# Forming the fourth power table in the modulation's loop, and sending its first loads without TensorE's count

## The chip, the cores and the metric

The kernel runs on one core of one Trainium2 chip. The metric is the device time of one execution in microseconds; the number for a kernel is the median of its runs. The profile is one more execution, recorded by the hardware profiler.

## What is computed

One transformer block over 4096 rows of 512 channels with a context of 3202 rows of 384 channels, in float32, followed by a quantised feed-forward with a convolution. The part that matters here:

```python
# c_t: attention over the context, top 32 of each row, averaged over 4 heads
x = layernorm(x_text, g_norm_in, b_norm_in)
scale_in, shift_in = jnp.split(c_t @ W_film_in + b_film_in, 2, axis=-1)
x = x * (1.0 + mod_gate * scale_in) + mod_gate * shift_in      # the modulation
# s4d: y = causal convolution of x with K, per channel, plus x * D_skip
dt = jnp.exp(log_dt)
A = A_re + 1j * A_im
dtA = dt[:, None] * A
dC = C * (jnp.exp(dtA) - 1.0) / A
powers = jnp.exp(dtA[:, :, None] * jnp.arange(L))
K = 2.0 * jnp.einsum('dn,dnl->dl', dC, powers).real
```

The kernel never forms all powers: for a part of 32 channels (16 pairs of channels, 64 states, real and imaginary part) it keeps a "power table" of the powers 0 to 128, and carries states from chunk to chunk of 128 rows. There are 16 such parts.

## The kernel before

The program is a row of stages with a barrier of all engines between most of them: `prepare`, `attention` with `modulate` in the same block, `s4d`, `feed_forward`, `bit_feed_forward`. Each engine has its own instruction stream, written out in order; semaphores (`wait_ge`, `then_inc`) are all that orders them against each other. SP's stream issues most DMAs, and its waits hold back every DMA that stands behind them.

**attention** works on 32 tiles of 128 rows. Its last steps: VectorE adds the heads of the last tile (L932, then L936, which raises `last_summed`), GpSimd's adds of the heads are L808 to L819, TensorE transposes the sum (L1106, raising `turned`) and multiplies with the context (L1116), ScalarE copies the product into `u` (L998) and stores it to `scratch_u` (L1001, raising `u_stored`).

**modulate** works on the same 32 tiles, two buffers each for u and xt. For tile n:
- SP loads `u` (L1225) after TensorE's count `u_turned` and `xt` (L1227) after VectorE's count `x_read`. `u_turned` and `x_read` are raised by 2 at the start of TensorE's and VectorE's own streams of this stage.
- TensorE turns u (L1380). ScalarE makes the high half of u in float32r (L1361), VectorE the low half (`low_u`, L1308).
- TensorE multiplies three combinations of high and low halves with the film weights (L1393, 9 products for each of two halves) and adds `fb_parts` (L1396).
- VectorE takes the row statistics of xt (L1302, L1304), ScalarE the root (L1357), VectorE the reciprocal (L1313), then `film`: L1315 with the first half and L1318 with the second, which writes X by channel and raises `film_read`.

In VectorE's stream each round is `low_u` and `stats_of` of the next tile and then `film` of this one. Rounds stand in a loop of two tiles (`Fori`). Ahead of the loop VectorE makes `wf_parts` (L1324 to L1333) and `fb_parts` from GpSimd's `fbg` (L1337, L1339), and only then the first `low_u`. `fbg` is made by GpSimd (L1255 to L1258) from `fb`, which SP loads (L1234) behind the first four loads of u and xt. Then SP loads `W` and `root` (L1236, L1237).

Meanwhile GpSimd forms `powers` and the first three power tables (L1265 to L1288). One step of a table is two products with W (L1275), a drain, a difference and a sum (L1278, L1279), a drain. A table has 12 steps: one of width 1 for power 128, then widths 1, 2, 4 and 8, and seven steps of 16 columns (levels of 16, 32 and 64 columns go in pieces of 16).

**s4d** goes over 16 parts. TensorE: `gather(g)` (turns table g, sums the kernel, gathers the input of each chunk), `spread(g)` (output). The order is gather 0, gather 1, then gather g + 2 and spread g. VectorE: `table(3)` first, then `carry(0, 1)` and `carry(1, 1)`, then for each pair of parts a table, a carry (L1624 to L1656) over both, a table. There are four table buffers, so `table(g)` waits for the output of part g - 4. `carry` waits for ScalarE's copies of the gathered input (`U_copied`, L1699).

Of the kernel before, what the change touches and what calls it, by code (L numbers as in the profile page):

```python
# [8 lines left out]
F32 = mybir.dt.float32  # L9
BF16 = mybir.dt.bfloat16  # L10
F32R = mybir.dt.float32r
I32 = mybir.dt.int32
U8 = mybir.dt.uint8
ALU = mybir.AluOpType
# [3 lines left out]
P = 128  # L18
# [47 lines left out]
def after(m, b):  # L66

    return (m + 1, 0) if b else (m, 1)
# [1111 lines left out]
def modulate(nc, sem, block, attended, const, a, W, root_table, powers, first_tables, X, dram, wide, passed_on):  # L1180
# [5 lines left out]
    with scope:  # L1186
        u = sb("mod_u", [P, 2, DV])
        xt = sb("mod_xt", [P, 2, D])
        minus = sb("mod_minus", [P, P])
        minus_r = sb("mod_minus_r", [P, P], F32R)  # L1190
# [4 lines left out]
        rstd = sb("mod_rstd", [P, 2])  # L1195
        uT = sb("mod_uT", [P, 2, 2, VC, P], F32R)
        M = sb("mod_M", [P, 2, 2, GP, PIECE])
        sb("mod_gap", [P, 1088])
        wf_parts = sb("mod_wf_parts", [P, 2, VC, 2 * D], F32R)
        fb_high = sb("mod_fb_high", [2, 2 * D], F32R)  # L1200
        fb_parts = sb("mod_fb_parts", [P, 2 * D], F32R)
        part = sb("mod_part", [P, 2, D])
        fb = part.rearrange("p b d -> p (b d)")[0:2]
# [15 lines left out]
        def _(sp):  # L1219
            def load(m, b):  # L1220
                n = 2 * m + b
                sp.wait_ge(s["u_turned"], n + 1)
                if n >= TILES - 4:
                    sp.wait_ge(attended["u_stored"], 16 * (n + 2))
                sp.dma_start(u[:, b], dram["u"][n * P:(n + 1) * P, :]).then_inc(s[f"uin{b}"], 16)  # L1225
                sp.wait_ge(s["x_read"], n + 1)
                sp.dma_start(xt[:, b], a["x_turned"][n * P:(n + 1) * P, :]).then_inc(s[f"xin{b}"], 16)  # L1227

            sp.wait_ge(attended["summed"], SCORE_CHUNKS * (TILES - 1))
# [3 lines left out]
            sp.wait_ge(attended["last_summed"], SCORE_CHUNKS)  # L1233
            sp.dma_start(fb[:], dram["fb"][1, :].partition_broadcast(2)).then_inc(s["fb_in"], 16)  # L1234
            sp.wait_ge(attended["turned"], SCORE_CHUNKS * TILES)
# [6 lines left out]
        def _(pool):  # L1242
            nc.gpsimd.memset(eps2[:], EPS * EPS)
# [4 lines left out]
            pool.wait_ge(attended["last_summed"], SCORE_CHUNKS)  # L1248
# [9 lines left out]
            nc.gpsimd.tensor_tensor(fbg[0:2, D:2 * D], fbg[0:2, D:2 * D], fb[:, D:2 * D], ALU.add).then_inc(s["fb_scaled"], 1)  # L1258
            pool.wait_ge(attended["turned"], SCORE_CHUNKS * TILES)
# [23 lines left out]
            for t, Q in enumerate(first_tables):  # L1283
# [13 lines left out]
        def _(dve):  # L1297
# [8 lines left out]
            def low_u(m, b):  # L1306
                dve.wait_ge(s["uT_high"], 2 * m + b + 1)
                nc.vector.tensor_tensor(uT[:, b, 1], tp[b][:, :, ::-1], uT[:, b, 0].bitcast(F32), ALU.subtract).then_inc(s["uT_ready"], 1)  # L1308
# [28 lines left out]
            nc.vector.tensor_copy(fb_high[:], fbg[0:2])  # L1337
            dve.drain()
            nc.vector.scalar_tensor_tensor(fb_parts[0:2], fb_high[:].bitcast(F32), is_low[:, 0:1], fbg[0:2], ALU.mult, ALU.subtract).then_inc(s["fb_ready"], 1)  # L1339
            low_u(0, 0)  # L1340
            stats_of(0, 0)
            with dve.Fori(0, TILES // 2 - 1) as i:
                for b in range(2):
                    low_u(*after(i, b))
                    stats_of(*after(i, b))
                    film(i, b)
            low_u(TILES // 2 - 1, 1)
            stats_of(TILES // 2 - 1, 1)
            film(TILES // 2 - 1, 0)
# [85 lines left out]
def s4d(nc, sem, const, a, W, root, powers, first_tables, X, dram, wide, passed_on):  # L1435
# [15 lines left out]
    with scope:  # L1451
        Q = first_tables + [sb("s4_Q3", [P, 2, GP, P + 1])]
# [36 lines left out]
        with nc.Block() as block:  # L1489
# [84 lines left out]
            def _(dve):  # L1574
# [98 lines left out]
                dve.sem_inc(s["Q_ready"], 3)  # L1673
                table(3)
# [1608 lines left out]
def xattn_ffn(nc, a, out):  # L3283
    whole = ExitStack()
    with whole:
# [60 lines left out]
        with nc.Block() as block:  # L3346
# [9 lines left out]
            first_tables.append(third_table)  # L3356
            modulate(nc, sem, block, attended, const, a, W, root, powers, first_tables, X, dram, wide, passed_on)
# [58 lines left out]
```

## Time and profile before

| | us |
|---|---|
| median of 3 runs (3888.87 to 3891.64) | 3889.6 |
| the profiled execution | 3883.47 |
| its span, first to last instruction | 3881.7 |

In the profiled execution attention runs until about 1810 us, the modulation from about 1809 to 1978, and s4d from 1979 to about 2470. A row of the order of time gives the start and the length of an instruction, or of several alike in a row (x7), and in brackets how long its engine stood idle before, and what released it. Names ending in q (SPq, ACTq) are the engine's own queue issuing a DMA.

### The profile page before, as it was taken

The numbers are of one execution on the slowest core, as the hardware profiler recorded it, in microseconds if no ns is written. First come the engines' busy times: TensorE is split into PE (matmuls) and PEld (weight loads), VectorE is DVE, ScalarE is ACT, GpSimd is POOL, SyncE is SP. The second block draws the span as 40 slices with busy tenths as digits, with TensorE's granted clock in tenths as the row PEclk, the third lists the DMA queues.
The fourth block names the chain that finished last, engine by engine and source line by source line (L and its number), as shares of the span: only waits on it lengthen the run. The fifth ranks groups of instructions, "written<-read, shape, count | busy, mean of one in ns | idle before, by whom it ended". The sixth has DMA issues, their size and how long they took to land. (4 is left out here: it accounts for less than half of the span.)

```text
span 3881.7 us, 54514 instructions
## 1 busy us (share of the span) xinstructions
PE 3191.9 (82%) x17202; PEld 2127.3 (55%) x17202; DVE 2952.2 (76%) x7412; ACT 2275.6 (59%) x2934; POOL 1625.6 (42%) x1324
## 2 busy tenths in 40 slices
PE   7648758887878578887998777689999999978998
PEld 3224334444444244445865555467777777766776
DVE  7799999999999999996668998434444434468898
ACT  4578778898888698883133333133333223357876
POOL 0025546565555365665810000013332333317775
PEclk9758878788888787888999998899999999989999
DMA  9710000000000000002224333633444333430212
GB/s 321 259 47 11 10 8 10 10 10 10 12 10 10 5 13 10 10 5 83 94 58 98 82 92 82 195 121 126 133 133 133 128 103 117 143 97 15 67 50 70
DMA packets 262025, 290.53 MB, mean 75 GB/s; under 512 B 53264, under 2 KB 175782, under 8 KB 260588
## 3 DMA queue, kind: packets, MB, share of 16 engines
q1 hardware_dynamic: 245320, 262.39, 22.1%
q0 software_dynamic: 3040, 14.94, 1.0%
q10 hardware_dynamic: 13380, 10.00, 0.8%
q8 instruction: 106, 1.74, 0.2%
q14 instruction: 179, 1.47, 0.1%
HBM read 218.82 MB, written 68.45 MB: 74 GB/s over the span
## 5 line engine op out<-in xcount | busy, mean ns | idle before, releaser
L1116 PE MATMUL up<-ctx,attnT 128*128 128x384 f32 (+1 forms) x1664 | 718.8, 588 | 44.0 <-ACT attnT L988 43.9
L1086 PE MATMUL score<-KT,q 64*128 64x512 f32 (+1 forms) x1792 | 386.9, 527 | 330.1 <-ACT S L948 240.1
L849 DVE MAX8 both_wide<-S 128x8 f32<-128x146 f32 (+1 forms) x2816 | 601.2, 295 | 43.8 <-ACT S L948 25.0
L808 POOL TENSOR_TENSOR S<-S 128x512 f32<-128x512 f32 (+1 forms) x224 | 424.5, 1927 | 355.0 <-DVE S L854 355.0
L1116 PEld LDWEIGHTS up<-ctx,attnT 128*128 128x128 f32 (+1 forms) x1664 | 367.6, 231 | 319.6 <-issue 158.8
L854 DVE SCALAR_TENSOR_TENSOR S<-S,both_wide 128x3202 f32<-128x3202 f32 x128 | 472.8, 3756 | 14.6 <-ACT both_wide L979 14.6
L1086 PEld LDWEIGHTS score<-KT,q 64*128 64x128 f32 x1792 | 175.7, 239 | 531.9 <-ACT S L948 396.0
L948 ACT ACTIVATE S<-score 128x1024 f32<-128x1024 f32 (+1 forms) x448 | 403.1, 931 | 91.6 <-PE score L1086 91.1
L2301 DVE TENSOR_TENSOR ff_gelu<-ff_whole,ff_gelu 128x512 fp32r<-128x512 f32 x128 | 100.6, 786 | 417.3 <-ACT ff_gelu L2538 417.3
L957 ACT ACTIVATE both_wide<-S,below 128x3202 bf16<-128x3202 f32 x128 | 379.6, 2966 | 41.3 <-DVE below L889 20.4
L979 ACT ACTIVATE both_wide<-S,ebias 128x3202 f32<-128x3202 f32 x128 | 376.2, 2963 | 23.9 <-DVE S L854 13.5
L2705 PE MATMUL both_acc<-ff_W,ff_gelu 128*128 128x512 f32 x1000 | 336.7, 397 | 0.0
L2537 ACT ACTIVATE ff_whole<-both_hidden,ff_b 128x512 f32<-128x512 f32 x128 | 87.8, 686 | 389.5 <-PE both_hidden L2690 389.2
L2690 PE MATMUL both_hidden<-ff_hT,both_W 128*128 128x512 f32 x1024 | 264.7, 400 | 5.8 <-ACT ff_gelu L2538 4.3
L815 POOL TENSOR_TENSOR S<-S 128x512 f32<-128x512 f32 (+1 forms) x217 | 243.7, 1163 | 6.8 <-issue 6.8
L2977 POOL TENSOR_TENSOR bf_silu<-bf_silu,both_wide 128x912 f32<-128x912 f32 (+1 forms) x67 | 177.5, 2689 | 112.6 <-ACT both_wide L3156 112.6
L2690 PEld LDWEIGHTS both_hidden<-ff_hT,both_W 128*128 128x128 f32 x1024 | 189.8, 189 | 48.2 <-ACT ff_gelu L2538 5.4
L2705 PEld LDWEIGHTS both_acc<-ff_W,ff_gelu 128*128 128x128 f32 x1000 | 188.7, 189 | 44.4
L819 POOL TENSOR_TENSOR S<-S 128x512 f32<-128x512 f32 (+1 forms) x217 | 207.6, 992 | 4.9 <-issue 4.9
L2705 PE MATMUL both_acc<-ff_w_low,ff_gelu 128*128 128x512 f32 x500 | 197.9, 396 | 0.0
L2122 POOL TENSOR_TENSOR both_wide<-both_wide 128x512 f32<-128x512 f32 x28 | 36.1, 1288 | 369.8 <-DVE ff_xt L2190 369.8
L1548 POOL TENSOR_SCALAR s_Kz<-root 64x16 f32<-64x16 f32 x64 | 25.2, 394 | 369.6 <-PE s_ksp L1773 366.4
(500 smaller groups left out, 6462.3 us busy)
## 6 DMA issues: line engine op xcount, KB each, us to landing
s_hankel<-scratch_K SPq DMA_DIRECT2D x128, 256.0 KB, 4.2
ff_w_low<-scratch_w1l SPq DMA_DIRECT2D x112, 256.0 KB, 2.7
ff_w_low<-scratch_w2l SPq DMA_DIRECT2D x112, 256.0 KB, 2.8
xt_prep<-in_x SPq DMA_DIRECT2D x8, 1024.0 KB
scratch_xt<-xt_prep SPq DMA_DIRECT2D x8, 1024.0 KB, 7.4
both_wide<-in_ffn_w_t POOLq DMA_DIRECT2D x8, 1024.0 KB, 11.2
q<-scratch_qt SPq DMA_DIRECT2D x128, 64.0 KB
mod_xt<-in_x_turned SPq DMA_DIRECT2D x32, 256.0 KB, 2.6
```

What stands on the lines that cost most here:

```text
L808: nc.gpsimd.tensor_tensor(S[:, b, 0, chunk(j)], S[:, b, 0, chunk(j)], S[:, b, 1, chunk(j)], ALU.add).then_inc(s["summed01"], 1)
L815: nc.gpsimd.tensor_tensor(S[:, b, 0, chunk(j)], S[:, b, 0, chunk(j)], S[:, b, 2, chunk(j)], ALU.add).then_inc(s["summed02"], 1)
L819: nc.gpsimd.tensor_tensor(S[:, b, 0, chunk(j)], S[:, b, 0, chunk(j)], S[:, b, 3, chunk(j)], ALU.add).then_inc(s["summed"], 1)
L849: nc.vector.max(cand[:, h, 8 * k:8 * k + 8], S[:, b, h, k * SEG:min((k + 1) * SEG, G)])
L854: nc.vector.scalar_tensor_tensor(S[:, b, h, :], S[:, b, h, :], tops[:, b, h, TOP - 1:TOP], E[:, h % 2, :], ALU.is_ge, ALU.mult).then_inc(s ...
L948: nc.scalar.activation(S[:, b, PAIRS_OF_HEADS[p], chunk(j)], score[bank(p, j)][:, :, 0:w], ACT.Copy).then_inc(s["score_copied"], 1)
L957: nc.scalar.activation(signs, S[:, b, h, :], ACT.Sign, bias=below[:, h:h + 1], accum_out=count[:, h:h + 1]).then_inc(s["counted"], 1)
L979: nc.scalar.activation(E[:, h % 2, :], S[:, b, h, :], ACT.Exp, bias=ebias[:, b, h:h + 1], scale=SCALE).then_inc(s["e_ready"], 1)
L1086: last = nc.tensor.matmul(score[bank(p, j)][:, e, 0:w], lhsT=q[at, b, part, h // 2, :], rhs=KT[at, h // 2, chunk(j)], start=(part == 0), s ...
L1116: last = nc.tensor.matmul(up[:, 0:DV], lhsT=attnT[0:w, e, c - 4 * g, :], rhs=ctx[0:w, c, :], start=(c == 0), stop=(c == GC - 1))
L2690: last = nc.tensor.matmul(fp[f % 2][:], lhsT=left, rhs=hT[:, h_part, c, :], start=(j == 0), stop=(j == len(terms) - 1))
L2705: last = nc.tensor.matmul(acc[:, k, :], lhsT=gelu[:, g_part, F % RING, k * P:(k + 1) * P], rhs=right, start=(f == 0 and j == 0), stop=(f = ...
```

## The change

- SP's stream of the modulation: `fb` is loaded first, after `last_summed`. Then SP waits for all of attention's transposes and the stores of u, and loads the first two tiles of u and xt. These two no longer wait for `u_turned`; tiles from 2 on do.
- A fourth table buffer is allocated for both stages. GpSimd still forms the first three tables; the fourth is formed by VectorE in the modulation. Its 12 steps are cut in two half steps each, the products and the sums. One half step stands behind the `film` of each of the tiles 1 to 24. VectorE's loop is written out, 31 rounds.
- Ahead of these rounds VectorE waits for the last store of u, and after tile 0 for W and root.
- In s4d `table(3)` is gone, and VectorE raises `Q_ready` by 4 at once.
- GpSimd's first memsets stand behind `last_summed`. Buffers are laid out in another order; `fb` and `fb_high` share memory with the tables' scratch.

```diff
-            sp.wait_ge(attended["summed"], SCORE_CHUNKS * (TILES - 1))
+            sp.wait_ge(attended["last_summed"], SCORE_CHUNKS)
+            sp.dma_start(fb, dram["fb"][1, :].partition_broadcast(2)).then_inc(s["fb_in"], 16)
+            sp.wait_ge(attended["turned"], SCORE_CHUNKS * TILES)
             sp.wait_ge(attended["u_stored"], 16 * (TILES - 3))
             load(0, 0)
             load(0, 1)
-            sp.wait_ge(attended["last_summed"], SCORE_CHUNKS)
-            sp.dma_start(fb[:], dram["fb"][1, :].partition_broadcast(2)).then_inc(s["fb_in"], 16)
-            sp.wait_ge(attended["turned"], SCORE_CHUNKS * TILES)
...
                 n = 2 * m + b
-                sp.wait_ge(s["u_turned"], n + 1)
+                if n >= 2:
+                    sp.wait_ge(s["u_turned"], n + 1)
...
+            pool.wait_ge(attended["last_summed"], SCORE_CHUNKS)
             nc.gpsimd.memset(eps2[:], EPS * EPS)
             nc.gpsimd.memset(minus[:], 0.0)
             nc.gpsimd.memset(is_low[:], 1.0)
             nc.gpsimd.memset(fbg[:], 0.0)
             pool.drain()
-            pool.wait_ge(attended["last_summed"], SCORE_CHUNKS)
...
-            for t, Q in enumerate(first_tables):
+            for t, Q in enumerate(first_tables[:3]):
...
             low_u(0, 0)
             stats_of(0, 0)
-            with dve.Fori(0, TILES // 2 - 1) as i:
-                for b in range(2):
-                    low_u(*after(i, b))
-                    stats_of(*after(i, b))
-                    film(i, b)
-            low_u(TILES // 2 - 1, 1)
-            stats_of(TILES // 2 - 1, 1)
-            film(TILES // 2 - 1, 0)
+            own = first_tables[3]
+            at = slice(GP * 3, GP * 4)
+            STEPS = [(LEVELS, 0, 1, P)] + [(level, first, min(1 << level, PIECE), (1 << level) + first)
+                                           for level in range(LEVELS) for first in range(0, 1 << level, PIECE)]
+
+            def products(k):
+                level, first, w, to = STEPS[k]
+                for half in range(2):
+                    nc.vector.tensor_tensor(own_M[:, half, :, :, 0:w], own[:, :, :, first:first + w],
+                                            W[:, level, half, at].unsqueeze(1).unsqueeze(3).broadcast_to([P, 2, GP, w]), ALU.mult)
+
+            def sums(k):
+                level, first, w, to = STEPS[k]
+                nc.vector.tensor_tensor(own[:, 0, :, to:to + w], own_M[:, 0, 0, :, 0:w], own_M[:, 1, 1, :, 0:w], ALU.subtract)
+                nc.vector.tensor_tensor(own[:, 1, :, to:to + w], own_M[:, 0, 1, :, 0:w], own_M[:, 1, 0, :, 0:w], ALU.add)
+
+            dve.wait_ge(attended["u_stored"], 16 * (TILES + 1))
+            for n in range(TILES - 1):
+                m, b = divmod(n, 2)
+                low_u(*after(m, b))
+                stats_of(*after(m, b))
+                film(m, b)
+                if n == 0:
+                    dve.wait_ge(s["tables_in"], 32)
+                    nc.vector.tensor_copy(own[:, :, :, 0], root_table[:, :, at])
+                k, half = divmod(n - 1, 2)
+                if 0 <= n - 1 < 2 * len(STEPS):
+                    dve.drain()
+                    if half == 0:
+                        products(k)
+                    else:
+                        sums(k)
             film(TILES // 2 - 1, 1)
...
-                dve.sem_inc(s["Q_ready"], 3)
-                table(3)
+                dve.sem_inc(s["Q_ready"], 4)
                 carry(0, 1)
                 carry(1, 1)
```

## Rows read from the trace of the kernel before

**Rows 1.** The page, busy time of each engine over the span.

```profile
PE 3191.9 (82%) x17202; PEld 2127.3 (55%) x17202; DVE 2952.2 (76%) x7412; ACT 2275.6 (59%) x2934; POOL 1625.6 (42%) x1324
```

**Rows 2.** Waits, 1780 to 1980 us: us in total, times, longest.

```profile
DVE X L1318 <- PE mod_film L1396: 52.1, 32, 1.6
```

**Rows 3.** Order of time at the hand-over; the last row is scratch_u's landing, 1800 to 1830.

```profile
1791.59 0.19 POOL L1249 MEMSET mod_minus<- 2x128 f32 x1 [3.68 <-DVE S L936]
...
1800.13 9.39 PE L1116 MATMUL up<-ctx,attnT 128*128 128x384 f32 x28
...
1806.17 0.33 SPq L1225 DMA_DIRECT2D mod_u<-scratch_u  x1
...
1807.96 0.29 SPq L1234 DMA_DIRECT2D mod_part<-scratch_fb  x1
...
1810.41 0.34 ACTq L1001 DMA_DIRECT2D scratch_u<-u  x1
1810.80 0.49 ACT L1361 ACTIVATE mod_uT<-mod_tp 128x384 fp32r<-128x384 f32 x1 [0.50 <-ACT u L998]
1811.00 1.28 POOL L1255 TENSOR_TENSOR third_table<-mod_part,both_wide 2x512 f32<-2x512 f32 x1 [15.20 <-DMA mod_part<-scratch_fb]
...
1814.92 0.68 DVE L1337 CAST mod_fb_high<-third_table 2x1024 fp32r<-2x1024 f32 x1 [10.72 <-POOL third_table L1258]
...
1816.88 0.54 DVE L1308 TENSOR_TENSOR mod_uT<-mod_tp,mod_uT 128x384 fp32r<-128x384 f32 x1
...
1817.47 4.21 PE L1393 MATMUL mod_film<-mod_wf_parts,mod_uT 128*128 128x512 f32 x9 [5.55 <-DVE mod_uT L1308]
...
1824.29 2.32 PE L1393 MATMUL mod_film<-mod_wf_parts,mod_uT 128*128 128x512 f32 x9
...
DMA to landing us min/median/max: 9.1/9.1/9.1
```

**Rows 4.** Stretches: busy time of engines, then granted clock, DMA share, GB/s.

```profile
1785.00:1790.00 5.00, 3.88 (x16) 1.99 (x15) 4.93 (x8) 1.51 (x3) 2.91 (x6) 1.00 0.33 123
...
1812.00:1817.40 5.40, 0.00 (x0) 0.00 (x0) 2.40 (x4) 0.00 (x0) 2.75 (x3) 0.50 0.93 352
1817.40:1821.70 4.30, 4.23 (x10) 3.36 (x11) 2.07 (x7) 1.95 (x3) 1.76 (x3) 0.52 0.27 103
```

**Rows 5.** Order of time of one round of the modulation, VectorE.

```profile
1962.19 1.18 DVE L1318 SCALAR_TENSOR_TENSOR X<-mod_part,mod_rstd,mod_film 128x512 f32 x1 [1.63 <-PE mod_film L1396]
...
1964.73 0.75 DVE L1315 SCALAR_TENSOR_TENSOR mod_part<-mod_xt,mod_mv,mod_film 128x512 f32<-128x512 f32 x1
...
1967.12 1.18 DVE L1318 SCALAR_TENSOR_TENSOR X<-mod_part,mod_rstd,mod_film 128x512 f32 x1 [1.64 <-PE mod_film L1396]
```

**Rows 6.** Single lines: ns min/median/max, first and last start, forms.

```profile
L932 DVE TENSOR_TENSOR S<-S x7: 280/1572/1576, 1779.1 to 1787.3; 128x512 f32<-128x512 f32 x6, 128x130 f32<-128x130 f32 x1
...
L936 DVE TENSOR_TENSOR S<-S x7: 285/684/693, 1787.6 to 1791.2; 128x512 f32<-128x512 f32 x6, 128x130 f32<-128x130 f32 x1
...
L1275 POOL TENSOR_TENSOR mod_M<-third_table,W x24: 268/1084/1093, 1904.5 to 1936.6; 128x512 f32<-128x512 f32 x14, 128x32 f32<-128x32 f32 x4, 128x64 f32<-128x64 f32 x2, 128x128 f32<-128x128 f32 x2
```

**Rows 7.** Order of time in s4d's table(3), VectorE, full steps.

```profile
1985.05 1.29 DVE L1585 TENSOR_TENSOR s_M<-s_Q,W 128x512 f32<-128x512 f32 x2
...
1986.42 0.42 DVE L1590 TENSOR_TENSOR s_Q<-s_M 128x256 f32<-128x256 f32 x1
...
1987.25 2.50 DVE L1585 TENSOR_TENSOR s_M<-s_Q,W 128x512 f32<-128x512 f32 x4
```

**Rows 8.** Order of time at the start of s4d.

```profile
1979.01 1.28 DVE L1596 COPY s_Q<-root 128x32 f32<-128x32 f32 x1 [1.42 <-PEq L3295]
...
1997.96 1.09 ACT L1699 ACTIVATE s_S<-s_stp 128x256 f32<-128x256 f32 x2 [0.43 <-PE s_stp L1786]
...
1999.58 0.76 DVE L1624 TENSOR_TENSOR s_M<-s_S,s_turn 128x256 f32<-128x256 f32 x2 [0.17 <-issue]
...
2038.57 0.20 DVE L1596 COPY both_wide<-root 128x32 f32<-128x32 f32 x1 [6.68 <-PE s_ytp L1831]
```

More of the change, by code:

```diff
@@ L1188, in modulate @@
         xt = sb("mod_xt", [P, 2, D])
-        minus = sb("mod_minus", [P, P])
-        minus_r = sb("mod_minus_r", [P, P], F32R)
+        M = sb("mod_M", [P, 2, 2, GP, PIECE])
+        fb = M.rearrange("p a b k w -> p (a b k w)")[0:2]
+        wf_parts = sb("mod_wf_parts", [P, 2, VC, 2 * D], F32R)
+        own_M = sb("mod_own_M", [P, 2, 2, GP, PIECE])
+        fb_high = own_M.rearrange("p a b k w -> p (a b k w)")[0:2].bitcast(F32R)
+        fb_parts = sb("mod_fb_parts", [P, 2 * D], F32R)
         eps2 = sb("mod_eps2", [P, 1])
@@ L1195, in modulate @@
         rstd = sb("mod_rstd", [P, 2])
+        minus = sb("mod_minus", [P, P])
         uT = sb("mod_uT", [P, 2, 2, VC, P], F32R)
[L1197 to L1201, printed above, removed]
+        minus_r = sb("mod_minus_r", [P, P], F32R)
         part = sb("mod_part", [P, 2, D])
-        fb = part.rearrange("p b d -> p (b d)")[0:2]
         wf = film_in_of(wide)
@@ L1258, in _ @@
             nc.gpsimd.tensor_tensor(fbg[0:2, D:2 * D], fbg[0:2, D:2 * D], fb[:, D:2 * D], ALU.add).then_inc(s["fb_scaled"], 1)
+            pool.drain()
             pool.wait_ge(attended["turned"], SCORE_CHUNKS * TILES)
@@ L1336, in _ @@
             dve.wait_ge(s["fb_scaled"], 1)
-            nc.vector.tensor_copy(fb_high[:], fbg[0:2])
+            nc.vector.tensor_copy(fb_high, fbg[0:2])
             dve.drain()
-            nc.vector.scalar_tensor_tensor(fb_parts[0:2], fb_high[:].bitcast(F32), is_low[:, 0:1], fbg[0:2], ALU.mult, ALU.subtract).then_inc(s["fb_ready"], 1)
+            nc.vector.scalar_tensor_tensor(fb_parts[0:2], fb_high.bitcast(F32), is_low[:, 0:1], fbg[0:2], ALU.mult, ALU.subtract).then_inc(s["fb_ready"], 1)
             low_u(0, 0)
@@ L1451, in s4d @@
     with scope:
-        Q = first_tables + [sb("s4_Q3", [P, 2, GP, P + 1])]
+        Q = first_tables
         S = sb("s4_S", [P, 2, 2, CHUNKS + 1, BOTH])
@@ L3356, in xattn_ffn @@
             first_tables.append(third_table)
+            first_tables.append(layer.enter_context(nc.sbuf_tensor("fourth_table", [P, 2, PART // 2, P + 1], F32)))
             modulate(nc, sem, block, attended, const, a, W, root, powers, first_tables, X, dram, wide, passed_on)
```

## Prediction

> **What bounds the kernel now.** I read first the page's busy shares, then the waits of the modulation (1780 to 1980 us), then the order of time at its two ends. No engine is full over the whole run [rows 1], so each stage has to be read alone. The change touches three places: the hand-over from attention to modulation, the modulation's loop, and the start of the stage behind it (S4D below).
>
> Hand-over. TensorE goes over from attention's last transposes to their products at 1800.13 us, and works on these until 1800.13 + 9.39 = 1809.5. SP's queue is held by the wait for u_turned, which TensorE raises when its instructions reach the modulation; the first u load goes out at 1806.17 and the load of fb, third behind it, at 1807.96. GpSimd has waited 15.2 us for it and starts at 1811.00; VectorE, free from 1804.2 on, waited 10.7 us for GpSimd, until 1814.92. VectorE's instructions stand in one order, so the low half of the first u, whose high half ScalarE had ready at 1810.80 + 0.49 = 1811.3, is made only at 1816.88, and TensorE's first film product starts at 1817.47 after a wait of 5.55 us [rows 3]. So fb ends last here. [...]
>
> Loop. From L1318 of one tile to L1318 of the next it is 4.93 us (1962.19 to 1967.12), and VectorE stands 1.64 us of it waiting for TensorE (52.1 us over the 32 tiles [rows 2]); TensorE is the bound [rows 5].
>
> S4D's start. VectorE forms the fourth table from 1979.01 until the first carry at 1999.58. Yet that carry needs ScalarE's copy, which ends at 1997.96 + 1.09 = 1999.05, and after both carries VectorE stands 6.68 us until TensorE has done the first spread (2038.57) [rows 8]. The fourth table ends last nowhere: it runs beside gather(0) on TensorE.
>
> **Part 1, the first loads.** SP now waits for last_summed (about 1791.6, where GpSimd's L1249 starts after VectorE's last sum [rows 3]), sends fb, waits until all of attention is turned (about 1800.3) and sends both tiles of u and xt, then W and root. fb takes about 3.0 us (1807.96 to 1811.00), so it lies there by 1795. GpSimd's four memsets move behind the same wait (an estimate: 1 to 2 us); with its cast of 4.0 us and three scalings of 1814.92 - 1811.00 = 3.9 us [rows 3] it is through at about 1801, or at 1806 if each meets VectorE's splitting of the weights, which then ends up to 4 us later than 1804.2. VectorE's two steps for fb take 1816.88 - 1814.92 = 2.0 us, so they end between 1806 and 1810. Next in line is then ScalarE's high half at 1811.3, since ScalarE copies attention's last context first, and TensorE finishes that only at 1809.5. The low half starts at 1811.3 instead of 1816.88: 5.6 us gained. The u loads go out 5.8 us earlier; they end last nowhere once TensorE is busy until 1809.5, so this half of the edit is worth nothing more by itself (a second u that lands before 1809.9 lets the second turn start about 1 us earlier, hidden behind ScalarE).
>
> The gap of TensorE shrinks from 5.5 us to about 1.5. Before the film products at 1817.47 the clock was low; but from 1785 to 1790, with 1.1 us of TensorE idle in it, 1.00 was granted [rows 4]. The first nine film products took 4.21 us, against 2.32 us for nine at full clock (1824.29) [rows 3]. If the clock stays up, that is 4.21 - 2.32 = 1.9 us more; ends 0 and 1.9, and I take 1.9, the gap of 1.5 being nearer to 1.1 than to 5.5.
>
> **Part 2, an added wait.** Ahead of the loop VectorE waits until attention's last u is stored. Behind it stands the low half of tile 1, and TensorE waits for that. The store goes out at 1810.41 and took 9.1 us to land [rows 3], but in a stretch in which the DMA engines were 0.93 busy with W and root (1812 to 1817.4) [rows 4]. With W and root sent 6 us earlier the engines are free by about 1813 (0.27 of the 4.3 us behind 1817.4 were still busy: 1818.6 before), and the store is through with them. TensorE wants the low half of tile 1 at about 1811.9 + 4.9 = 1816.8. I cost it at 0; if the store still took 9.1 us it would land at 1819.5 and TensorE would stand 3.3 us.
>
> **Part 3, the table in the loop.** 12 steps make 24 half steps, in tiles 1 to 24: of these 7 steps are of full width. A pair of full products takes 1986.42 - 1985.05 = 1.37 us with its drain, the two sums 1987.25 - 1986.42 = 0.83 [rows 7]. In front of each half step comes a drain that lets L1318 run out, 0.2 at most. Two tiles thus get 1.37 + 0.83 + 0.4 = 2.6 us. VectorE needs 1964.73 + 0.75 - 1962.19 = 3.3 us a tile today and 0.1 for its drain [rows 5]: two tiles 6.8 + 2.6 = 9.4, against TensorE's 9.86. By itself it fits, with 0.45 us left for two tiles. The five small steps fit easily.
>
> But it doesn't run by itself: GpSimd forms its tables until about 1939 (its last product starts at 1936.6 [rows 6]) with instructions that read two operands from SBUF. The nearest rows are the two adds of the same shape at attention's end: L932, beside GpSimd's adds, took a median 1.572 us, its seven starts spread over 1779.1 to 1787.3, one every 1.37; L936, with GpSimd idle, took 0.684, from 1787.6 to 1791.2, one every 0.60 [rows 6]. So an instruction that always meets one of GpSimd's loses 0.77 us. The present loop shows none of this; but its three long instructions read one tensor from SBUF and one from PSUM, or one alone. The new ones all read two from SBUF. Of the four in two tiles, the bounds are 0 and 4 x 0.77 = 3.1 us. The products of GpSimd and its sums of half the size alternate, with drains between them, and VectorE comes to them at random after 3.3 us of other work, so I take a third of the upper end, 1.0 us. That is 0.55 us above the room, over 7 pairs 3.8. TensorE doesn't stand for all of it: there are two buffers, and the low half of the next but one tile is there about 3.3 us after L1318 starts where it is wanted at 4.9, so a lag of 1.5 us is free, and some of the rest falls where GpSimd pauses. I take 1.5 us lost; ends 0 and 7 x (9.4 + 3.1 - 9.86) - 1.5 = 17.0.
>
> [...]
>
> GpSimd loses what VectorE takes: some 12 us at most, its tables ending at about 1945 instead of 1939, with the loop's end near 1970. Hidden.
>
> VectorE's loop is written out (31 tiles instead of two in a loop). The trace doesn't show the cost; the written-out S4D shows single "issue" gaps (0.17 us in front of the first carry [rows 8]). Ends 0 and 0.1 us a tile; taken as part of the 1.5.
>
> **Part 4, S4D's start.** 20 us of VectorE's work go, and no wait of another engine: the carry can start 1999.05 instead of 1999.58, and the 6.68 us wait behind it grows to 7.2. GpSimd's weights for gather run without VectorE beside them, at most 0.3 us earlier for TensorE. I take 0.3.
>
> **Sum.** -5.6 - 1.9 + 0 + 1.5 - 0.3 = -6.3 us. The profiled execution has a span of 3881.7 and took 3883.5 in all; it would be 3877.2. It lay 6.1 us below the median of the runs, 3889.6, from which I start: 3883.3 us.
>
> **Rivals.**
> Full contention (slower). Every full half step meets GpSimd at each instruction, as L932 did. +17.0 in the loop: 3889.6 - 7.8 + 17.0 = 3898.8. For it: L932 itself, and that GpSimd goes from table to table without a wait for another engine. Against: L932's partner issued nothing but adds of full size, and here VectorE is away for most of a tile. It decides from 0.45 us lost per instruction on (7 x (9.4 + 1.8 - 9.86) - 1.5 = 7.9 against 7.8 gained). 0.08.
> The wait for the store. It lands as late after issue as before: +3.3, 3886.6. 0.08.
> The start doesn't move: something in front of the first film, fb's chain or u, still ends at 1817. Then only parts 3 and 4 are left: 3889.6 + 1.5 - 0.3 = 3890.8. Against it, the times above leave 1.3 us or more. 0.06.
> The table was on the path after all: S4D starts its chain of tables with 20.6 us less in front, 3883.3 - 20.3 = 3863.0. Against it stands the 6.68 us wait. 0.03.
> The clock stays low through the first film: part of the forecast, 3885.2.
>
> **How the numbers follow.** The forecast holds 0.75, with its parts 1 and 3 open: from 3880.0 (contention and added wait 0, and 2 us of other drift) to 3887. With the store and the unmoved start inside, and 1.5 us of scatter of the medians (3888.87 to 3891.64) on each side, the range is 3878.0 to 3892.5. A measurement can tell 0.2% from no change, 7.8 us: 3881.8 and 3897.4. The forecast lies 1.5 us on the inner side of that bound, so of its 0.75 I give 0.29 to faster; with the table's rival that is 0.32. Slower: full contention, 0.07, rounded to 0.08. The same: 0.60.
>
> **What would show it.** The first film product at about 1811.9 with a wait of TensorE below 2 us and granted clock 1.00 behind it; GpSimd's wait for fb gone; L1585's counterparts in the loop with medians between 0.68 and 1.4 us; VectorE's wait for TensorE in the loop down from 1.64 us to near nothing in tiles 11 to 24, and back to 1.64 behind them; GpSimd's last table later in relation to its start. In S4D the wait of VectorE for the first spread still there, and longer, and the distance from the first transposes to the second stage's fifth table unchanged. A first film at 1811.9 with a modulation as long as before would mean that contention ate the gain; a shorter S4D would mean that I misread its start.

## The result, and the profile after

The kernel after takes 3883.3 us, median of 21 runs (3879.1 to 3888.7), the kernel before 3889.1 (21 runs, 3885.5 to 3896.3). The ratio is 0.9986, 95% interval 0.9980 to 0.9992: 5.8 us less, interval 3.1 to 7.8. That is real and below the 0.2% named as the bound: "the same", at the predicted number. Two terms of the sum were still wrong, and one was right only because two errors in it cancel. One run of 3969.4 us, in the slow state, is left out of the medians below (kernel e5).

One profiled execution alone doesn't show such a gain. Its busy shares are those of [rows 1]:

```profile
span 3885.5 us, 54327 instructions
...
PE 3191.8 (82%) x17202; PEld 2128.7 (55%) x17202; DVE 2960.0 (76%) x7412; ACT 2275.1 (59%) x2934; POOL 1633.8 (42%) x1324
```

Its span is 3.8 us longer than that of before, 3881.7, though the median is shorter: attention's last products started 5.2 us later in it (1805.35 against 1800.13). Of these, 3.2 us were there before the hand-over's first instruction (L932 starts at 1782.3 against 1779.1), and 2.0 us went to a lower clock of TensorE on the way (0.50 from 1791.6 to 1795.4, last section). So stages are measured inside, from marks next to them.

**The hand-over**, in order of time, kernel after (start, duration, engine, line, operation, tiles, idle time before and its releaser); it is to be read beside [rows 3]:

```profile
1794.76 0.26 SPq L1231 DMA_DIRECT2D mod_M<-scratch_fb  x1
...
1799.23 1.26 POOL L1255 TENSOR_TENSOR third_table<-mod_M,both_wide 2x512 f32<-2x512 f32 x1 [0.23 <-issue]
...
1805.55 0.34 SPq L1226 DMA_DIRECT2D mod_u<-scratch_u  x1
...
1809.15 1.27 DVE L1340 SCALAR_TENSOR_TENSOR mod_fb_parts<-mod_own_M,mod_is_low,third_table 2x1024 fp32r<-2x1024 f32 x1
...
1815.63 0.34 ACTq L1001 DMA_DIRECT2D scratch_u<-u  x1
1816.02 0.49 ACT L1386 ACTIVATE mod_uT<-mod_tp 128x384 fp32r<-128x384 f32 x1 [0.50 <-PE mod_tp L1405]
1816.55 0.56 DVE L1309 TENSOR_TENSOR mod_uT<-mod_tp,mod_uT 128x384 fp32r<-128x384 f32 x1 [6.12 <-ACT mod_uT L1386]
...
1817.16 3.86 PE L1418 MATMUL mod_film<-mod_wf_parts,mod_uT 128*128 128x512 f32 x9 [1.61 <-DVE mod_uT L1309]
```

fb goes out at 1794.76 and is scaled without a wait; VectorE is through with it at 1809.15 + 1.27 = 1810.4 and then waits 6.12 us for ScalarE's high half, where before GpSimd's fb held it past that half. From ScalarE's start on that half to the first film product it was 1817.47 - 1810.80 = 6.67 us; now 1817.16 - 1816.02 = 1.14.

**The stretches** around it, with [rows 4]: each engine's busy time, then granted clock, DMA share, GB/s:

```profile
1815.60:1817.20 1.60, 0.04 (x1) 0.04 (x1) 0.65 (x2) 0.49 (x1) 0.00 (x0) 0.95 0.91 329
1817.20:1821.00 3.80, 3.80 (x10) 3.04 (x11) 1.57 (x4) 1.95 (x3) 2.56 (x4) 0.57 0.26 97
```

During the gap the granted clock is still 0.95, yet over the products behind it 0.57 (0.50 until 1820.6). Nine take 3.86 us, not the 2.32 of the nine at 1824.29 in before [rows 3], over which 1.00 was granted.

**The loop**, VectorE, with [rows 5]: four starts of L1319 (formerly L1318) in tiles with steps of full width, and the half steps between them:

```profile
1883.68 1.17 DVE L1319 SCALAR_TENSOR_TENSOR X<-mod_part,mod_rstd,mod_film 128x512 f32<-128x512 f32 x1
1884.94 0.68 DVE L1356 TENSOR_TENSOR fourth_table<-mod_own_M 128x256 f32<-128x256 f32 x1
1885.54 1.31 DVE L1357 TENSOR_TENSOR fourth_table<-mod_own_M 128x256 f32<-128x256 f32 x1
...
1888.95 1.17 DVE L1319 SCALAR_TENSOR_TENSOR X<-mod_part,mod_rstd,mod_film 128x512 f32<-128x512 f32 x1
1890.22 1.90 DVE L1351 TENSOR_TENSOR mod_own_M<-fourth_table,W 128x512 f32<-128x512 f32 x2
...
1894.22 1.17 DVE L1319 SCALAR_TENSOR_TENSOR X<-mod_part,mod_rstd,mod_film 128x512 f32<-128x512 f32 x1
...
1904.76 1.18 DVE L1319 SCALAR_TENSOR_TENSOR X<-mod_part,mod_rstd,mod_film 128x512 f32<-128x512 f32 x1
```

No L1319 waits for TensorE here. Four tiles take 1904.76 - 1883.68 = 21.1 us, a pair 10.54, where TensorE alone sets 9.86. The second sum took 1.31 us, against 0.42 in [rows 7]; a pair of products 1.90, against 1.29. These two pairs are longer than the average. All seven full steps lie between these two starts:

```profile
1877.74 1.17 DVE L1319 SCALAR_TENSOR_TENSOR X<-mod_part,mod_rstd,mod_film 128x512 f32<-128x512 f32 x1 [0.81 <-PE mod_film L1421]
1949.92 1.18 DVE L1319 SCALAR_TENSOR_TENSOR X<-mod_part,mod_rstd,mod_film 128x512 f32<-128x512 f32 x1
```

That is 72.2 us for seven pairs, 10.31 a pair on the average, and no L1319 between them waits for TensorE. Over the modulation and its neighbourhood (1780 to 1980) the wait is, with [rows 2] (us in total, times, longest):

```profile
DVE X L1319 <- PE mod_film L1421: 16.2, 15, 1.5
```

Before it was 52.1 us in 32 tiles; now VectorE's slack is used up in 17 of them.

**Single lines** (ns min/median/max, first and last start), with [rows 6]: GpSimd's products take what they took (median 1087 against 1084), single ones now up to 1522. The last one starts 4.2 us later than the 1936.6 of before, although the first started 1.6 us earlier (1831.9 against 1833.5), so GpSimd's tables take 5.8 us longer:

```profile
L1276 POOL TENSOR_TENSOR mod_M<-third_table,W x24: 270/1087/1522, 1905.7 to 1940.8; 128x512 f32<-128x512 f32 x14, 128x32 f32<-128x32 f32 x4, 128x64 f32<-128x64 f32 x2, 128x128 f32<-128x128 f32 x2
```

The stage's length is read from such a row: from the first film product to the last start of L1319. Before and after:

```profile
L1318 DVE SCALAR_TENSOR_TENSOR X<-mod_part,mod_rstd,mod_film x32: 1075/1182/1201, 1824.3 to 1976.5; 128x512 f32 x30, 128x512 f32<-128x512 f32 x2
```

```profile
L1319 DVE SCALAR_TENSOR_TENSOR X<-mod_part,mod_rstd,mod_film x32: 1071/1178/1199, 1823.6 to 1978.1; 128x512 f32<-128x512 f32 x32
```

Before 1976.5 - 1817.5 = 159.0; after 1978.1 - 1817.2 = 160.9. So the stage is 1.9 us longer.

**S4D's start**, with [rows 8]: VectorE still waits for the first spread, 7.23 us instead of 6.68:

```profile
2040.48 0.20 DVE L1621 COPY both_wide<-root 128x32 f32<-128x32 f32 x1 [7.23 <-PE s_ytp L1855]
```

From the last L1319 to here it is 2040.48 - 1978.14 = 62.3 us, before 2038.57 - 1976.52 = 62.05. VectorE's 20 us of table went out of S4D and its start isn't shorter.

### The profile page after: what moved, and what is told of

Read it like the earlier page. It is cut to its first block and busy times, and to the rows that moved or that the text cites. A ratio compares the mean times of both kernels' runs of the same rounds, so it can differ in the third digit from the quotient of the medians.

```text
span 3885.5 us, 54327 instructions
## 1 busy us (share of the span) xinstructions
PE 3191.8 (82%) x17202; PEld 2128.7 (55%) x17202; DVE 2960.0 (76%) x7412; ACT 2275.1 (59%) x2934; POOL 1633.8 (42%) x1324
## 5 line engine op out<-in xcount | busy, mean ns | idle before, releaser
L1116 PE MATMUL up<-ctx,attnT 128*128 128x384 f32 (+1 forms) x1664 | 713.8, 584 | 42.3 <-ACT attnT L988 42.3
L1116 PEld LDWEIGHTS up<-ctx,attnT 128*128 128x128 f32 (+1 forms) x1664 | 364.5, 229 | 316.6 <-issue 157.9
```

What stands on the lines that cost most here:

```text
L1116: last = nc.tensor.matmul(up[:, 0:DV], lhsT=attnT[0:w, e, c - 4 * g, :], rhs=ctx[0:w, c, :], start=(c == 0), stop=(c == GC - 1))
```

## The experiments

"Hand-over" is the time from the start of attention's last product (L1116) to the first film product, "nine" the duration of the first nine film products, "stage" the length as above; these three are of one profiled execution each. (The recorded expectations of e1 to e3 count the stage to the end of the last L1319, 1.1 us more: 160.1 for before, 162.1 for after.) "To before" is the median minus that of the kernel before on the same chip. A median has a standard error of nearly 1 us, so differences of two medians below some 2.5 us tell nothing by themselves.

| kernel | median us (runs) | to before | ratio, 95% interval | hand-over | nine | stage |
|---|---|---|---|---|---|---|
| before | 3889.1 (21) | | | 8.5 | 4.21 | 159.0 |
| after | 3883.3 (21) | -5.8 | 0.9986 (0.9980 to 0.9992) | 2.9 | 3.86 | 160.9 |
| e0: after, again | 3882.9 (11) | -5.9 | 0.9986 (0.9977 to 0.9995) | 2.9 | 3.82 | 160.9 |
| e1: loads only | 3882.2 (11) | -7.0 | 0.9981 (0.9972 to 0.9990) | 2.9 | 3.88 | 158.7 |
| e2: table only | 3889.8 (11) | +0.5 | 1.0001 (0.9992 to 1.0010) | 9.5 | 3.92 | 159.9 |
| e3: GpSimd silent | 3880.9 (10) | -8.3 | 0.9979 (0.9969 to 0.9988) | 2.9 | 3.87 | 158.7 |
| e4: before, no fourth table | 3889.9 (11) | +0.7 | 1.0004 (0.9995 to 1.0013) | 8.4 | 4.21 | 159.4 |
| e5: steps in thirds | 3882.2 (10) | -6.6 | 0.9985 (0.9975 to 0.9994) | 2.9 | 3.86 | 159.0 |
| e6: after, gap filled | 3883.1 (11) | -5.7 | 0.9989 (0.9980 to 0.9998) | 2.9 | 2.34 | 159.2 |
| e8: loads only, gap filled | 3880.0 (11) | -8.8 | 0.9978 (0.9969 to 0.9987) | 2.9 | 2.33 | 157.1 |
| e10: e8 again | 3881.1 (10) | -8.9 | 0.9977 (0.9968 to 0.9986) | 2.9 | 2.34 | 157.1 |
| e7: thirds, gap filled | 3884.8 (11) | -5.2 | 0.9985 (0.9976 to 0.9994) | 2.9 | 2.34 | 157.2 |
| e11: e7 again | 3881.1 (11) | -7.5 | 0.9981 (0.9972 to 0.9990) | 2.9 | 2.35 | 157.2 |
| e9: before, no fourth table | 3889.5 (11) | -0.5 | 0.9996 (0.9987 to 1.0005) | 8.6 | 4.13 | 158.9 |

The theory on trial: all of the gain is the hand-over's, since fb no longer ends last; the table in the loop gives some back because VectorE's new instructions take longer beside GpSimd's; and the 20 us that leave S4D are worth nothing. The rivals: the gain comes from S4D, or the loop loses by something else than contention (the written-out loop, drains, VectorE's own need).

### The early loads alone

The kernel after without the table in the loop; S4D forms it as before.

```
-                if 0 <= n - 1 < 2 * len(STEPS):
+                if False:
...
-                dve.sem_inc(s["Q_ready"], 4)
+                dve.sem_inc(s["Q_ready"], 3)
+                table(3)
```

> The changed kernel with the fourth table put back at the start of S4D, so that only the first loads differ from the kernel before. My theory (the gain is the hand-over's, the table only costs): first film product 2.5 us after attention's last product instead of 7.9; modulation from first film product to last L1319 about 159.8 us, 2.2 less than with the table in it (162.1) and 0.35 less than before (160.1); median 5.5 to 6 us below before, at or below the changed kernel. Rival (the table's move is what gains, the loads are hidden): median within 1 us of before.

7.0 us gained, no less than by the whole change. The hand-over is 5.6 us shorter. The stage, in the same kind of row as above, is 1976.3 - 1817.65 = 158.7, with the written-out loop and all else but the half steps in it, so neither the unrolling nor the added wait costs anything that can be seen:

```profile
1817.65 3.88 PE L1417 MATMUL mod_film<-mod_wf_parts,mod_uT 128*128 128x512 f32 x9 [1.61 <-DVE mod_uT L1309]
```

```profile
L1319 DVE SCALAR_TENSOR_TENSOR X<-mod_part,mod_rstd,mod_film x32: 1074/1180/1196, 1824.1 to 1976.3; 128x512 f32<-128x512 f32 x32
```

### The table alone

The kernel after with SP's order of loads as before.

```
-                if n >= 2:
-                    sp.wait_ge(s["u_turned"], n + 1)
+                sp.wait_ge(s["u_turned"], n + 1)
...
             sp.wait_ge(attended["last_summed"], SCORE_CHUNKS)
-            sp.dma_start(fb, ...)
-            sp.wait_ge(attended["turned"], SCORE_CHUNKS * TILES)
             sp.wait_ge(attended["u_stored"], 16 * (TILES - 3))
             load(0, 0)
             load(0, 1)
+            sp.dma_start(fb, ...)
+            sp.wait_ge(attended["turned"], SCORE_CHUNKS * TILES)
```

> The changed kernel with SP's order and waits of before at the hand-over, so that only the fourth table has moved. My theory: first film product again about 8 us after attention's last product, loop about 2.2 us longer than before, S4D unchanged to 0.3 us: median 1.5 to 3 us above before. Rival (the table's 20 us at the head of S4D were on the path): below before by more than 5 us.

+0.5 us (interval -3.1 to +3.9): no gain. It is less of a loss than the 1.5 to 3 us expected. TensorE waits 6.87 us in front of its first film product again:

```profile
1821.45 3.92 PE L1417 MATMUL mod_film<-mod_wf_parts,mod_uT 128*128 128x512 f32 x9 [6.87 <-DVE mod_uT L1308]
```

The stage is 0.9 us longer than before, 1.2 more than e1's; the 2.2 that were expected for the loop did not come, and why the table costs less here than in after is open. Together e1 and e2 give the gain to the loads, and none of it to S4D. They moved the load of fb and those of the first u and xt together. That fb's is the one that counts is read from the rows (GpSimd's wait of 15.20 us for it, and VectorE's for GpSimd [rows 3]) and wasn't tried by itself.

### GpSimd silent in the loop

The kernel after, where GpSimd's three tables are not computed (one memset each); VectorE does all that it does after.

```
-                g.tensor_copy(Q[:, :, :, 0], root_table[:, :, at])
-                pool.drain()
-                step(Q, at, LEVELS, 0, 1, P)
-                for level in range(LEVELS):
...
+                g.memset(Q[:], 0.0)
+                pool.drain()
```

> The changed kernel with GpSimd's steps of the first three tables left out (a memset each instead), so that VectorE's half steps run with GpSimd idle; the tables are not computed. Theory that the loop is longer by contention with GpSimd: two full products take 1.3 us together and the sums 0.75 again, a pair of tiles 9.85 us, and first film to last L1319 is 159.8 us. Rival (the half steps' own length, the drains or the written-out loop make it longer): a pair stays above 10.3 us and the modulation at 162.

The stage falls from 160.9 to 158.7, e1's length. In order of time, VectorE, a pair of tiles with full steps:

```profile
1881.81 1.17 DVE L1314 SCALAR_TENSOR_TENSOR X<-mod_part,mod_rstd,mod_film 128x512 f32<-128x512 f32 x1 [0.35 <-PE mod_film L1416]
1883.07 0.42 DVE L1351 TENSOR_TENSOR fourth_table<-mod_own_M 128x256 f32<-128x256 f32 x1
1883.41 0.42 DVE L1352 TENSOR_TENSOR fourth_table<-mod_own_M 128x256 f32<-128x256 f32 x1
...
1885.08 0.13 DVE L1309 RECIPROCAL mod_rstd<-mod_rstd 128x1 f32<-128x1 f32 x1
1885.12 0.73 DVE L1311 SCALAR_TENSOR_TENSOR mod_part<-mod_xt,mod_mv,mod_film 128x512 f32<-128x512 f32 x1
1886.74 1.17 DVE L1314 SCALAR_TENSOR_TENSOR X<-mod_part,mod_rstd,mod_film 128x512 f32<-128x512 f32 x1 [0.89 <-PE mod_film L1416]
1888.00 1.29 DVE L1346 TENSOR_TENSOR mod_own_M<-fourth_table,W 128x512 f32<-128x512 f32 x2
...
1891.67 1.17 DVE L1314 SCALAR_TENSOR_TENSOR X<-mod_part,mod_rstd,mod_film 128x512 f32<-128x512 f32 x1 [0.36 <-PE mod_film L1416]
```

The same instructions, and VectorE waits for TensorE again, 0.35 and 0.89 us in a pair of 1891.67 - 1881.81 = 9.86. Its own need is thus 9.86 - 1.24 = 8.6 us. The pairs of after shown above, 10.54, hold 10.54 - 8.6 = 1.9 us of contention, 0.48 for each of the four instructions; over all seven steps it is 10.31 - 8.6 = 1.7 us a pair, 0.42 each. Contention with GpSimd is shown as the cause; the rival that the table is too much work for the loop by itself is out.

What lost time are instructions that read two tensors from SBUF. L1319, with one input from PSUM, took a median of 1178 ns in after and 1182 in before, and 1170 here, where it is L1314 and GpSimd is silent. In what way an instruction of GpSimd holds up one of VectorE is not shown; single losses in after go up to 0.9 us (1.31 against 0.42).

### The same work in smaller pieces

The kernel after, with a full step in three tiles (one product, the other, the two sums) and steps under width 8 in one.

```
+                PLAN += [[p, q]] if w < 8 else [[p], [q]] if w < PIECE else [[p0], [p1], [q]]
...
-                if 0 <= n - 1 < 2 * len(STEPS):
-                    dve.drain()
-                    if half == 0:
-                        products(k)
-                    else:
-                        sums(k)
+                if 1 <= n <= len(PLAN):
+                    for piece in PLAN[n - 1]:
+                        dve.drain()
+                        piece()
```

> The changed kernel with each full step in three tiles (one product, the other product, both sums) instead of two, and the four smallest steps in one tile each: the same instructions, in tiles 1 to 27. Theory that VectorE's sum over two tiles (10.5 us beside GpSimd, where TensorE needs 9.86) is what lengthens the loop: one tile now gets at most 0.25 + 0.60 + 0.77 = 1.6 us for a product, so the loop is TensorE's again, 158.7 to 159.2 us against 160.9, and the median lies 1.5 to 2.2 us below the changed kernel. Rival (TensorE waits for something else that the half steps bring, as the loads of xt): stays at 160.5 or more.

The stage is 159.0, 1.9 us shorter than e0's on the same chip. Tiles in which VectorE is late and tiles in which it waits now alternate:

```profile
1888.37 1.18 DVE L1319 SCALAR_TENSOR_TENSOR X<-mod_part,mod_rstd,mod_film 128x512 f32<-128x512 f32 x1
...
1893.00 1.19 DVE L1319 SCALAR_TENSOR_TENSOR X<-mod_part,mod_rstd,mod_film 128x512 f32<-128x512 f32 x1 [0.34 <-PE mod_film L1423]
```

The step still meets GpSimd, but the third tile adds 4.93 us of TensorE's time to a step's room and only some 3.1 of VectorE's old work (an estimate): 1.24 + 4.93 - 3.1 = 3.1 us of room instead of 1.24. The median, 3882.2, lies 0.7 us below e0's 3882.9 and so doesn't show the 1.9 us; it is as far off as medians scatter.

### S4D without the fourth table

The kernel before, with the fourth table not computed at all (a memset of its tile in place of the steps). If the 20 us were worth anything, they would show here.

```
-                dve.sem_inc(s["Q_ready"], 3)
-                table(3)
+                v.memset(Q[3][:], 0.0).then_inc(s["Q_ready"], 4)
```

> The kernel before with table(3) left out of S4D (one memset of its buffer instead) and nothing put in its place; the fourth table is not computed. My theory: VectorE's wait for the first spread stays and is about 7 us, the start of the next table stays 61 us behind the modulation's end, median within 1 us of before. Rival (those 20 us are on the path, or part of them is): median below before by 5 to 20 us.

+0.7 us, which looks like proof and isn't. The memset of 4128 elements stands in front of the count that TensorE's first gather waits for, and TensorE stood 6.84 us there, against 2.45 before:

```profile
1981.82 3.50 DVE L1673 MEMSET s_Q<- 128x4128 f32 x1 [2.17 <-PEq L3294]
1985.37 1.97 PE L1759 MATMUL s_tp<-ident,both_wide 128*128 128x128 f32 x8 [6.84 <-DVE s_Q L1673]
```

So the experiment put a wait of its own where it took one away, and was done again with three counts given first:

```
-                table(3)
+                v.memset(Q[3][:], 0.0).then_inc(s["Q_ready"], 1)
```

> The kernel before without table(3), as e4_no_fourth, but with the first three tables released ahead of the memset, so that TensorE's first gather doesn't wait for it (in e4_no_fourth it stood 4.4 us longer). The fourth table is not computed. My theory: S4D's start doesn't depend on the fourth table; VectorE stands about 7 us longer in all, the next table starts 61 to 62 us behind the modulation's last L1318, median within 1.5 us of before. Rival (part of the 20 us is on the path, and e4_no_fourth's delay covered it): median 3 us or more below before.

-0.5 us (interval -5.1 to +1.9), and VectorE stands where the table's work was, with ScalarE's copy as the releaser, and waits for the first spread behind it as before:

```profile
1983.69 3.50 DVE L1674 MEMSET s_Q<- 128x4128 f32 x1 [2.26 <-issue]
...
2002.77 0.76 DVE L1624 TENSOR_TENSOR s_M<-s_S,s_turn 128x256 f32<-128x256 f32 x2 [15.59 <-ACT s_S L1699]
...
2042.35 0.20 DVE L1596 COPY both_wide<-root 128x32 f32<-128x32 f32 x1 [7.33 <-PE s_ytp L1831]
```

Of the 20 us, 15.6 are idle time again at once. From the last L1318 (1980.35) to the second stage's first table it is 2042.35 - 1980.35 = 62.0 us, against 62.05 before, and this settles it more closely than the median. The table ended last nowhere.

### After once more, beside its variants

> The changed kernel again, beside its variants on the same chip. 5 to 7 us below before; first film product to last L1319 160.9 us from start to start.

-5.9 us, as the first time. In this profile VectorE's added wait shows: VectorE stands 2.23 us for attention's last store in front of the second tile's low half.

```profile
1818.74 0.56 DVE L1309 TENSOR_TENSOR mod_uT<-mod_tp,mod_uT 128x384 fp32r<-128x384 f32 x1 [2.23 <-DMA scratch_u<-u]
```

TensorE wants that half about 4 us after the low half of the first, when the first nine film products take 3.82 us at a granted clock of 0.57, and it isn't late: the stage is 160.9 again. The store landed 4.5 us after issue here and 3.7 in the other profile of after, where VectorE waited for ScalarE instead; before it took 9.1 [rows 3].

### TensorE kept busy in the gap

Ten transposes of the identity between TensorE's second turn and its first film product. Their output goes to a bank that the next film overwrites.

```
             turn_u(0, 1)
+            for _ in range(10):
+                nc.tensor.transpose(fp[1][:, 0, 0:P], const["ident"][:], const["ident"][:])
             film(0, 0, first=True)
```

> The changed kernel with ten transposes of the identity on TensorE between the turns of the first two u and the first film product, about 1.5 us that fill its gap of 1.6. Theory that the clock is low over the first film products because TensorE stood in front of them: granted 1.00 there, nine products in 2.3 us instead of 3.86, and 1.5 us less in the stage. Rival (the low clock comes from what lay further back, or the transposes don't count): still 3.8 us for nine, and 0 to 0.3 us lost.

Order of time of TensorE, then the stretch of the first film products:

```profile
1815.27 1.25 PE L1426 MATMUL mod_film<-ident 128*128 128x128 f32 x10
1817.05 2.34 PE L1418 MATMUL mod_film<-mod_wf_parts,mod_uT 128*128 128x512 f32 x9 [0.53 <-DVE mod_uT L1309]
```

```profile
1817.00:1819.20 2.20, 2.15 (x9) 1.80 (x10) 0.77 (x2) 1.27 (x1) 1.91 (x4) 1.00 0.33 119
```

Granted clock 1.00 instead of 0.57, nine products in 2.34 us instead of 3.86, the stage 1.7 us shorter (159.2). The median, -5.7, doesn't show it. So the same edit was made to e1, where no table disturbs the loop:

> The early loads alone, with the fourth table at S4D's start as before, and the ten transposes in TensorE's gap. If both theories hold, it beats both kernels: 2.2 + 1.5 us below the changed kernel, about 9.5 us below before. If the gap's clock can't be had, 7 us below before, as the early loads alone.

-8.8 us, the best of all, with the stage at 157.1, 1.6 below e1's:

```profile
1815.99 2.33 PE L1417 MATMUL mod_film<-mod_wf_parts,mod_uT 128*128 128x512 f32 x9 [0.52 <-DVE mod_uT L1309]
```

> The same kernel as e8_loads_busy, on the chip of the two others, to see whether its median of 3880.0 holds and how it stands to e7_both, from which it differs by where the fourth table is formed. Both theories: within 1.5 us of e7_both if the place of the table is worth nothing once it fits; e7_both lower by 3 us or more if its removal from S4D's start is worth something.

-8.9 us the second time. It is faster than before by more than after is: the ratio's interval is 0.9968 to 0.9986, against 0.9980 to 0.9992 for after, and the two just overlap. On the chip on which e8 and e0 both ran, the medians are 3880.0 and 3882.9, 2.9 us apart with a standard error of some 1.2; e10 repeats it on another chip. The 3 us are likely, and small.

### Thirds and the busy gap together

e5 with e6's edit. If the table costs nothing once it is spread, this should equal e8.

> The changed kernel with the table in thirds and TensorE's gap filled. If the two gains of the stage add up: first film to last L1319 157.1 us, as e8_loads_busy, and a median 3 to 4 us below the changed kernel, about 3880. Rival (the stage's gain is given back behind it, as the medians of e5_thirds and e6_busy_gap suggest): 157.1 us in the stage but a median of 3882 to 3883.

> The same kernel as e7_both, once more. Its modulation was as short as that of e10_loads_busy_again, but its median lay 5.2 us below before and not 8.9. Theory that this was the scatter of medians of 11 runs: now 7 us or more below before. Rival (the table in the modulation costs something outside the modulation that one profile doesn't show): again 5 to 6 us below.

The stage is 157.2 both times, e8's 157.1; the medians are -5.2 and -7.5 against -8.8 and -8.9. The mean difference is 2.5 us, with a standard error of some 1.2. Whether the table in the modulation costs something outside of the stage stays open: the profiles show no place for it.

## Why the prediction was right or wrong

**What bounds, and the hand-over: right.** fb ended last, and goes. Predicted 5.6 us gained, fb's chain through between 1806 and 1810, and ScalarE's high half next. Measured 6.67 - 1.14 = 5.5 (hand-over 8.5 to 2.9), the chain through at 1810.4 in a run in which attention ends 5 us late, and that half next. e1 and e2 show it from both sides. The rival in which the start doesn't move is out.

**The clock after a short gap: wrong.** The step that failed is "the gap of 1.5 being nearer to 1.1 than to 5.5". In order of time, the kernel before, the idle time of the stretch chosen as nearest is one wait of 1.03 us, behind a row of products and ahead of eight transposes:

```profile
1784.08 3.26 PE L1116 MATMUL up<-ctx,attnT 128*128 128x384 f32 x9
1788.38 1.26 PE L1106 MATMUL turn<-ident,S 128*128 128x128 f32 x8 [1.03 <-DVE S L936]
```

Behind that wait 1.00 was granted (1788.4 to 1793); behind 1.61 us, with only 0.87 of transposes right ahead, 0.57. Which of the two differences decides wasn't tried, and other waits of TensorE just ahead show that length alone can't be what decides. In before and in after, the same two transposes and 28 products follow a wait for ScalarE of the same length:

```profile
1774.90 0.66 PE L1106 MATMUL turn<-ident,S 128*128 128x128 f32 x2 [2.84 <-ACT attnT L988]
1775.36 11.98 PE L1116 MATMUL up<-ctx,attnT 128*128 128x384 f32 x28
```

```profile
1778.10 0.41 PE L1106 MATMUL turn<-ident,S 128*128 128x128 f32 x2 [2.83 <-ACT attnT L988]
1778.35 9.39 PE L1116 MATMUL up<-ctx,attnT 128*128 128x384 f32 x28
```

Behind it 0.50 was granted in before (1775 to 1780) and 1.00 in after (1778 to 1783). So a forecast of the clock behind a wait of 1 to 3 us, made from one stretch of one trace, was a guess either way. Of the 1.9 us, 4.21 - 3.86 = 0.35 came. The lower bound, 0, was in the range, and the case with the clock low was named, at 3885.2. e6 and e8 show that the term is real: with the gap closed to 0.5 us the nine products take 2.34, and the stage loses 1.6 to 1.7 us.

**The added wait: right, at 0.** It does hold VectorE, by 2.2 us in e0, and nobody waits for it. The rival (+3.3) is out; the store landed in 3.7 and 4.5 us.

**The table in the loop: the size right, two terms in it wrong.** Predicted +1.5; measured 160.9 - 159.0 = 1.9 longer, although the first nine products took 0.35 less, so 2.2. VectorE's own need for two tiles was put at 9.4 us and is 8.6: the drains cost 0.09 (1881.81 + 1.17 = 1882.98, next start 1883.07), not the up to 0.2 and 0.1 of the author's estimate; and the written-out loop, costed at 0 to 0.1 us a tile, saves 0.17, since from L1313's start to L1315's it took 1964.73 - 1964.52 = 0.21 before and 1885.12 - 1885.08 = 0.04 in e3. The row of before:

```profile
1964.52 0.13 DVE L1313 RECIPROCAL mod_rstd<-mod_rstd 128x1 f32<-128x1 f32 x1
```

The room was thus 1.24 us and not 0.45. Contention was put at 1.0 a pair ("a third of the upper end") and is 1.7 on the average, more than half of it. The excess, 10.31 - 9.86 = 0.45 a pair, came out near the 0.55 of the prediction, 3.2 us over 7 pairs instead of 3.8, of which 2.2 reach TensorE's path. One term too pessimistic hid one too optimistic.

**Full contention (slower): not that far.** The prediction let it decide from 0.45 us per instruction on, and 0.42 was reached on the average, 0.48 in the pairs shown. Yet the loss in the loop is 2.2 us and not near the gain, since the point was worked out with the room of 0.45. With 1.24 it lies higher: 7 x (8.6 + 4c - 9.86) - 1.5 = 5.9, the gain without the table, gives c = 0.58, an estimate, and a rough one (at 0.42 the same formula gives 1.4 us where 2.2 were lost). Contention was the right thing to fear, and some 0.15 us per instruction short of deciding.

**S4D: right that it is worth nothing.** The wait for the first spread grew to 7.2, as predicted. The 0.3 us gained there did not show (62.3 against 62.05, the wrong way, by less than profiles differ). The rival with the table on the path (3863.0) is out by e2, by e9 and by after itself.

**The sum.** By the profiles -5.5 - 0.35 + 2.2 + 0.3 = -3.4 us; by the medians -5.8 (3.1 to 7.8 less). The clock's missing 1.5 us should have put the time at 3885 or above, inside the range. So the exact hit is partly luck. The profiles' sum lies inside the interval of the medians, near its end of 3.1, but e0 measured -5.9 again, and the 2.4 us between sum and median are not explained. Attention's last part doesn't explain them: from the transposes behind L936 to the start of the last products (1788.38 to 1800.13) it takes 11.75 us in before and e9, 13.85 in e4, which has before's code too, and 13.2 to 13.8 in all the others.

**The ranges and chances.** The range, 3878.0 to 3892.5, held it; between "faster" and "the same" the time fell on the inner side of the bound, as forecast.

## What to carry to other kernels

Work moved off one stage into the idle time of another is worth nothing if it ended last nowhere in the old one, and in the new one it can cost where it meets another engine's instructions, as here 0.42 us for each beside GpSimd's; measure the idle time with the contention in it, and spread the work in pieces smaller than the slack of one round. Look first at what a queue holds back by its order: here the whole gain was in the early loads, by the rows in one of 8 KB that stood behind four others and a wait. Where a short gap of TensorE ahead of a burst can't be closed, try to fill it; here that took 1.6 to 1.7 us off the stage.

## What the runs showed of the hardware

- In after, with a single gap of 1.61 us between busy work on both sides, TensorE was granted 0.95 during the gap and 0.57 over the 3.8 us behind it (0.50 until 1820.6); the granted clock there was 0.56 or 0.57 in e0, e1, e3 and e5 too. All five profiles with such a gap and no filler (after, e0, e1, e3, e5) had nine products in 3.82 to 3.88 us, hardly better than after a gap of 5.55 (4.21) or 6.87 (3.92); a gap of 1.03 us in attention was followed by 1.00 (1788.4 to 1793). 1.25 us of transposes in the gap, which left 0.5 us, gave nine products in 2.33 to 2.35 us and a granted clock of 1.00 in all five profiles that had them (e6, e7, e8, e10, e11).
- The same wait with the same work around it was followed by 0.50 in one execution and by 1.00 in another. After the 2.84 us in attention (2.83 in after) the 28 products took 11.98 us in before, where 0.50 was granted until 1780, and 9.39 in after, where it was 1.00. Where they were done early, the wait for VectorE behind them was longer, 3.84 instead of 1.03 us, and was followed by 0.50 (1791.6 to 1795.4): eight transposes in 1.97 us instead of 1.26 and eight products in 4.41 instead of 2.85. That is the 2.0 us of attention's late end, and it moves from execution to execution.
- Beside GpSimd's products of 1.087 us a VectorE instruction that reads two tensors from SBUF lost 0.42 us on the average of the seven full steps, while single ones (the sum of 1.31 us) lost 0.9; GpSimd's tables took 5.8 us longer, where the prediction named 12 at most.
- A store of 192 KB landed 9.1 us after issue when the loads of W and root had been issued 1.7 us ahead of it (DMA share 0.93 [rows 4]), and 3.7 when they had been issued 7.8 us ahead, although the share was still 0.91 in the first 1.6 us behind it. The other profiles with early loads have 3.1 to 4.5.
